# Eleven warm-up products, a Toeplitz load on another queue and five steps moved in a two-layer gated block on one core

## The reference

```python
x = x + tanh(g_xattn[0]) * L0_xattn(ctx, ctx, layernorm(x), ssm_kernel, D, 8)
x = x + tanh(g_ffn[0]) * L0_ffn(layernorm(x), w1, w2, w3)      # hidden 1408
x = x + tanh(g_xattn[1]) * L1_xattn(layernorm(x), ctx, mask)
x = x + tanh(g_ffn[1]) * L1_ffn(layernorm(x), w1, w2, w3)      # hidden 2048
```

## Time and profile before

| what | us |
|---|---|
| median of 3 executions | 703.06 (702.85 to 703.75) |
| the profiled execution, its own time | 704.2 |
| its span, first to last instruction | 702.1 |
| PE busy | 691.6 |
| VectorE busy | 587.6 |
| ScalarE busy | 378.3 |
| GpSimd busy | 270.9 |

### The profile page before, as it was taken

How to read it: one execution, slowest core, us unless ns; L and a number is a source line. 1 busy time by engine, 2 the same in 40 slices (tenths; PEclk the granted TensorE clock), 3 DMA queues, 4 the chain that set the end, 5 groups by cost and what they waited for, 6 DMA issues and landing times.

```text
span 702.1 us, 9602 instructions
## 1 busy us (share of the span) xinstructions
PE 691.6 (99%) x3228; PEld 394.6 (56%) x3228; DVE 587.6 (84%) x1066; ACT 378.3 (54%) x574; POOL 270.9 (39%) x413
## 2 busy tenths in 40 slices
PE   9999999999999999999999999999999999999997
PEld 8777777777544444567654444444444444444445
DVE  4998888999999998658976999888988888888891
ACT  3255885383569898748477544344344334434340
POOL 5779778888766563546600001111100111110000
PEclk9999999999999999999999999999999999999999
DMA  8763464434179889998150434343422334331234
GB/s 293 252 219 116 127 243 132 149 114 121 38 150 193 184 190 193 211 311 345 38 144 15 61 76 90 91 90 76 90 50 57 91 90 91 76 80 44 72 77 106
DMA packets 140593, 90.98 MB, mean 130 GB/s; under 512 B 119040, under 2 KB 119552, under 8 KB 140544
## 3 DMA queue, kind: packets, MB, share of 16 engines
q1 hardware_dynamic: 138816, 86.35, 46.7%
q0 software_dynamic: 1200, 3.93, 1.8%
q10 hardware_dynamic: 528, 0.09, 0.1%
HBM read 53.04 MB, written 8.47 MB: 88 GB/s over the span
## 4 chain that ended last, share of the span: by engine, by line
PE 75%; DVE 10%; POOL 4%; issue 3%; DMA 3%; ACT 3%; SPq 1%; POOLq 0%; ACTq 0%; DVEq 0%
PE psum L854 28%; PE psum L699 15%; PE psum L886 14%; PE psum L781 5%; PE psum L837 3%; PE psum L793 3%; PE psum L815 3%; DMA phase_space<-phase_space 1%; DMA x_sb<-x_between 1%; DVE ln_bn L277 1%; PE psum L870 1%; PE psum L711 1%; DVE phase_space L1309 1%; DMA phase_space<-in_ctx 1%; DVE phase_space L1203 1%
## 5 line engine op out<-in xcount | busy, mean ns | idle before, releaser
L854 PE MATMUL psum<-phase_space 128*128 128x512 f16 x1024 | 223.9, 379 | 1.2 <-DMA phase_space<-phase_space 1.1
L854 PEld LDWEIGHTS psum<-phase_space 128*128 128x128 f16 x1024 | 99.9, 98 | 123.6 <-issue 1.7
L699 PE MATMUL psum<-phase_space 128*128 128x288 f32 x640 | 161.1, 407 | 0.2
L699 PEld LDWEIGHTS psum<-phase_space 128*128 128x128 f32 x640 | 119.0, 190 | 31.3 <-ACT phase_space L960 1.2
L675 POOL DMA_DIRECT2D out<-x_sb x15 | 9.3, 620 | 303.4 <-DVE x_sb L1390 303.4
L886 PE MATMUL psum<-phase_space 128*128 128x512 f16 x480 | 105.7, 379 | 0.0
L1150 ACT ACTIVATE phase_space<-psum,b_scalars 128x512 f32<-128x512 f32 x64 | 43.5, 682 | 80.1 <-PE psum L854 78.1
L781 PE MATMUL psum<-phase_space 128*128 128x512 bf16 (+1 forms) x384 | 79.0, 361 | 0.5 <-DVE phase_space L1251 0.5
L886 PEld LDWEIGHTS psum<-phase_space 128*128 128x128 f16 x480 | 47.0, 98 | 56.6
L1156 ACT ACTIVATE phase_space<-phase_space,magic 128x1024 f32<-128x1024 f32 x32 | 36.4, 1148 | 77.2 <-DVE phase_space L1369 77.2
L1354 DVE SCALAR_TENSOR_TENSOR phase_space<-psum,b_scalars,phase_space 128x512 f32<-128x512 f32 x64 | 47.7, 747 | 25.4 <-ACT phase_space L1150 25.4
(11 more groups left out here) (120 smaller groups left out, 1019.6 us busy)
## 6 DMA issues: line engine op xcount, KB each, us to landing
phase_space<-in_L_weights SPq DMA_DIRECT2D x24, 512.0 KB, 5.8
phase_space<-in_L_weights SPq DMA_DIRECT2D x12, 704.0 KB, 7.3
phase_space<-kpad SPq DMA_DIRECT2D x14, 512.0 KB, 4.2
phase_space<-in_context_heads SPq DMA_DIRECT2D x15, 384.0 KB, 5.2
x_sb<-in_x_tiles SPq DMA_DIRECT2D x16, 256.0 KB, 4.8
phase_space<-in_context_turned SPq DMA_DIRECT2D x8, 512.0 KB, 6.5
x_between<-x_sb SPq DMA_DIRECT2D x16, 256.0 KB
x_sb<-x_between SPq DMA_DIRECT2D x16, 256.0 KB, 7.5
```

The source lines that it names most:

```text
L699: return nc.tensor.matmul(at(bank(4 * hh + lo), 0, [[64, B], [1, NP]]), toep[n % 2][:, hh, (lo - li) * P:(lo - li + 1) * P], kv[n % 2][:, ...
L854: last = nc.tensor.matmul(bank(2 * (m % 3) + w), fb_qT[n % 2][:, kk % 2, kk // 2, :], b_wT[w][:, kk // 2, c * 512:(c + 1) * 512], start=(k ...
```

## The change

It has these parts.

- `warm_up` runs 11 constant products in place of 17.
- The first Toeplitz half is issued by ScalarE's queue as its first load, and d_first by SP in the place that the half had. The order of the other loads stays.
- On ScalarE, in tile 1 of the first FFN, silu (1,1) stands ahead of the rounding of hidden tile 0 instead of behind it.
- Sign chunk 11 moves from the end of stage 1 (`NBA` 12 to 11) to behind the exp of step 0 of stage 2.
- SP issues memories 0 and 1 ahead of the turn of hidden tile 15 instead of behind it and the store of tile 13.
- VectorE's statistics of tile 15 of stage 2 move from step 9 to step 10.
- The down product of tile 0 of the last stage, with the wait for all signs, stands after the chunks of tile 1 instead of tile 2. The down product of tile 1 stays after tile 3.

```diff
@@ -313,10 +313,10 @@
         B_FFN = {1: 5, 3: 6, 5: 7, 7: 8, 8: 9, 9: 10, 10: 11, 11: 12, 12: 13, 13: 14}
         ROWS_FFN = {0: 0, 2: 1, 4: 2, 6: 3, 14: 4}
         RELOAD_FFN = {11: (0,), 12: (1,), 13: (2,), 14: (3,), 15: (4, 5)}
-        NBA = 12
-        SIGN_STEP = {3: 12, 5: 13, 6: 14, 7: 15, 8: 16, 13: 17, 15: 18}
+        NBA = 11
+        SIGN_STEP = {0: 11, 3: 12, 5: 13, 6: 14, 7: 15, 8: 16, 13: 17, 15: 18}
         C_EARLY = {13: (0,), 14: (1, 2), 15: (3,)}
-        C_STEP = {0: (4,), 1: (5,), 2: (6,), 3: (7,), 5: (8,), 6: (9, 10), 7: (11, 12), 8: (13, 14), 9: (15,)}
+        C_STEP = {0: (4,), 1: (5,), 2: (6,), 3: (7,), 5: (8,), 6: (9, 10), 7: (11, 12), 8: (13, 14), 10: (15,)}
         VALID_STEP = {7: 0, 9: 1}
         NEG_STEP = {4: 0, 6: 1, 8: 2, 10: 3}
 
@@ -348,11 +348,6 @@
                     rows = (kpad if n >= 2 else taps_in)[n * G:n * G + G, :]
                     sp.dma_start(toep[n % 2], bass.AP(rows.tensor, rows.offset, [[1, P], [TAP, G], [1, L]])
                                  ).then_inc(s_tp[n % 2], 16)
-
-                def load_first_toeplitz(hh, s_done):
-                    row = taps_in[hh:hh + 1, :]
-                    sp.dma_start(toep[0][:, hh, :], bass.AP(row.tensor, row.offset, [[1, P], [1, L]])
-                                 ).then_inc(s_done, 16)
 
                 def load_weight(w, j):
                     if w == 2:
@@ -415,10 +410,12 @@
                     sp.dma_start(at_mem[b], ctx_in[b].rearrange("(u p) l -> p u l", p=P)).then_inc(c_mem[b], 16)
 
                 sp.dma_start(cx_sb[0][:, 0:NCX // 2], cx[0][:, 0:NCX // 2]).then_inc(s_cfirst, 16)
-                load_first_toeplitz(0, s_tfirst)
+                sp.dma_start(d_first[:, :], dskip[0:2 * G].rearrange("(a n) -> a n", a=1).to_broadcast([P, 2 * G])
+                             ).then_inc(s_tfirst, 16)
                 sp.dma_start(cx_sb[0][:, NCX // 2:NCX], cx[0][:, NCX // 2:NCX]).then_inc(s_cx[0], 16)
                 load_x(0)
-                load_first_toeplitz(1, s_tp[0])
+                row = taps_in[1:2, :]
+                sp.dma_start(toep[0][:, 1, :], bass.AP(row.tensor, row.offset, [[1, P], [1, L]])).then_inc(s_tp[0], 16)
                 load_x(1)
                 load_context(1)
                 load_toeplitz(1)
@@ -447,6 +444,9 @@
                         turn_x(n + 2 - NT)
 
                 for t in range(NT + 1):
+                    if t == NT:
+                        load_memory(0)
+                        load_memory(1)
                     if t >= 1:
                         turn_hidden(t - 1)
                     if t < NT - 2:
@@ -459,9 +459,7 @@
                         load_b(B_FFN[t])
                     for i in RELOAD_FFN.get(t, ()):
                         reload(i)
-                load_memory(0)
                 reload(6)
-                load_memory(1)
                 store_between(NT - 2)
                 store_between(NT - 1)
                 reload(7)
@@ -707,7 +705,7 @@
 
                 def warm_up():
                     pe.wait_ge(s_const, 2)
-                    for _ in range(17):
+                    for _ in range(11):
                         nc.tensor.matmul(bank(7)[:, 0:P], ones[:, :], ones[:, :], start=True, stop=True)
 
                 def first_conv():
@@ -935,9 +933,10 @@
                         pe.wait_ge(g_xT[n % 2], 16 * (n // 2 + 1))
                     for c in range(2 if n == 0 else 0, NCB):
                         b_chunk(n, c)
-                    if n == 2:
+                    if n == 1:
                         pe.wait_ge(s_bs, NBC)
-                    if 2 <= n < NT - 2:
+                        b_down(0)
+                    if 3 <= n < NT - 2:
                         b_down(n - 2)
                     if n == 2:
                         pe.wait_ge(t_red, 2)
@@ -1071,8 +1070,8 @@
                         act.wait_ge(g_xT[n % 2], 16 * (n // 2))
                     nc.scalar.activation(fb_qp[n % 2][:, 0, :], fb_q[n % 2], ACT.Copy).then_inc(g_hi, 1)
 
-                act.dma_start(d_first[:, :], dskip[0:2 * G].rearrange("(a n) -> a n", a=1).to_broadcast([P, 2 * G])
-                              ).then_inc(s_tfirst, 16)
+                row = taps_in[0:1, :]
+                act.dma_start(toep[0][:, 0, :], bass.AP(row.tensor, row.offset, [[1, P], [1, L]])).then_inc(s_tfirst, 16)
                 square_first(0)
                 square_first(1)
                 act.dma_start(kp_sb, taps_in).then_inc(s_kin, 16)
@@ -1110,9 +1109,11 @@
 
                 for t in range(NT):
                     a_silu(t, 0)
-                    if t >= 1:
+                    if t >= 2:
                         a_round_h(t - 1)
                     a_silu(t, 1)
+                    if t == 1:
+                        a_round_h(0)
                     if 1 <= t < NT - 2:
                         a_round_x(t + 2)
                     a_silu(t, 2)
```

## The result

The changed kernel takes 711.32 us, the median of 6 runs (710.62 to 714.17), against 703.12 (702.85 to 703.99, 6 runs) for the kernel before: ratio 1.0121, 95% interval 1.0103 to 1.014. It is slower by 8.2, where 3.9 was forecast, and 711.3 lies above the range.

The account below looks back on a forecast made before the run. TensorE bounds the kernel, busy 691.6 of 702.1 us, so only its gaps count. -0.65-0.65+2.1-0.44+3.5=+3.9: 708.1 us profiled, 706.9 as a median; range 703.6 to 709.8.

Parts of the forecast that it names:

- The start: First stage: shorter warm-up and earlier Toeplitz half start TensorE 0.6 sooner; -0.65 us, ends 0 and -1.3.
- The silu: Tile 1, first FFN: silu fits ScalarE's idle time, its chain ends sooner and closes the 210.31 gap; -0.65 us.
- Sign chunk and memories: Around 293 to 305 us: copy gap shrinks, but memories queued ahead delay the turn of hidden tile 15; +2.1 us net.
- so it waits about 3.2: 0.7 won, 3.2 lost, 0.39 won: Before down product 15: TensorE waits for the late tile, less gaps won at the copy and at 305.10; net +2.1 us.
- Statistics of tile 15: Stage 2: one statistics pair leaves VectorE's busy stretch, closing the gap ended by the exp; -0.44 us, ends -0.44 and 0.
- The early down product: Last stage: TensorE waits 1.7 for hidden tile 0, and the turn of x 3 moves by 3.5; +3.5 us.
- the 2.5 at which the forecast was to fall: Last stage: the forecast falls if the gaps near 392 and before tile 3 sum to less than 2.5 us.
- The four parts that gain: Start -0.65, silu -0.65, sign chunk 0.7 won at the copy, statistics of tile 15 -0.44 us.
- Rival 3: Start: shorter warm-up leaves TensorE idle, first convolution partly at half pace; up to 3.4 us more, 710.3; chance 0.09.
- Rival 1: First FFN: memories do not hold the turn of hidden tile 15; that part -0.4, sum +1.2, 704.3 us; chance 0.14.

Follow-up runs that it names:

- the wait is filled: Changed kernel with the last stage's first down product back behind tile 2, plus 12 constant products ahead of down product 15 of the first FFN: 703.68 us.
- the three fills: Changed kernel with 12, 11 and 12 constant products at the waits before down product 15, the early down product and tile 3: 709.14 us, ratio 1.0081.

## Why the prediction was wrong

**The start** (forecast -0.65): -0.62 by the end of the first stage, but in part by luck. The first convolution started 0.30 sooner (7.04, ended by GpSimd's pairs) and not 0.6, and VectorE's first products 0.22 sooner. The remaining 0.4 is a wait of PE's at 28.67 in the profiled execution of before:

```profile
28.67 0.63 PE L688 MATMUL psum<-ident,phase_space 128*128 128x128 f32 x4 [0.45 <-DVE phase_space L1212]
```

It is absent after the change, but also in the runs with the silu alone and with the down product alone, which leave the start as it was. The Toeplitz move, from which half a microsecond was expected, gives 0.1 of 1.6. The counts of 5 and 6 in the earlier trace rows are not the pace either, since a matmul counts in every stretch that it touches; the 1.3 for the removed matmuls held (5.07 for 6.38).

**The silu** (-0.65): 0.76 in the profile and 1.1 alone. The reasoning for the gap at 192, and the new wait at the first down product (0.63 for "about 0.5"), held. That the gap at 210 hangs on the silu's chain was wrong: it closed with the warm-up alone, where the chain is as it was.

**Sign chunk and memories** (+2.1): the mechanism was right, a wait of 2.75 for the 3.2 forecast, landing 6.0 after issue for the 6.5 of the earlier trace rows. What failed is the step "so it waits about 3.2: 0.7 won, 3.2 lost, 0.39 won": it prices a wait at its own length and puts the matmuls behind it at full pace without a reason. Down product 15 ran at the 1.2 GHz level behind it, 1.55 more. By medians the memories cost 3.7 (704.99 against 701.27), of which 2.4 are left when the wait is filled (703.68); the prediction has 3.2 less 0.39, 2.8. The 0.7 of the sign chunk did not come alone (703.86).

**Statistics of tile 15** (-0.44): the gap closed and nothing replaced it; 0.73 in the profile, and 0.9 alone, with an interval (0.1 to 1.4) that takes in the 0.44.

**The early down product** (+3.5): 5.9 in the profile, 5.6 alone, and 6.8 by medians in the version without the early memories. The two gaps came to 5.3, far from the 2.5 at which the forecast was to fall. PE waits 2.47 for the 1.7 forecast, because the second pair lands in up to 3.5 and not in the 2.7 that was taken. The rest is the same failed step: 1.68 of slow matmuls, which push the scales, the low halves and the turn of x 3 as well. The wait before tile 3 was forecast at 2.7 and is 2.79.

**The sum.** The four parts that gain came out as forecast in their sum, -2.4 by medians for -2.4 (-0.65-0.65-0.7-0.44). Part of that is luck, since singly they measured 1.6, 1.1, nothing and 0.9. The miss of 4.3 is in the other two: 3.7 for 2.8 and 6.8 for 3.5. The step that failed is the same in both. No term held the matmuls that run at half pace behind a wait of more than 2 us, 1.55 and 1.68 in the profile; by medians the three fills take back 2.2 to 2.7.

As a sum from the profile: of the other terms the waits of the last stage came out 0.9 larger than forecast (2.47+1.73 for 1.7+1.64), the wait at down product 15 0.45 smaller, and the gains 0.5 larger (3.3 for 2.8). From 3.9 these lead to 7.1, within 0.4 of the 6.7 of the span. The step from 6.8 to 8.2 is the place of the two profiled executions among their own runs: the prediction took 1.1 off on both sides, but the changed kernel's profiled execution lies 0.3 below its median. Rival 3 had the mechanism, but only at the start, where it decided nothing (the first convolution takes 5.09 for 5.02). Rival 1 adds up to +1.4 and not +1.2, which changes nothing.

The rows to see it were there: the kernel before has no wait over 1.06 on which to read the clock, but its last matmul ends at 698.0 and its own table then reads:

```profile
701.00:702.00 1.00, 0.00 (x0) 0.00 (x0) 0.00 (x0) 0.00 (x0) 0.00 (x0) 1.00 0.00 0
702.00:703.00 1.00, 0.00 (x0) 0.00 (x0) 0.00 (x0) 0.00 (x0) 0.00 (x0) 0.66 0.00 0
703.00:704.00 1.00, 0.00 (x0) 0.00 (x0) 0.00 (x0) 0.00 (x0) 0.00 (x0) 0.50 0.02 8
```

The clock falls some 4.3 us after TensorE stops; in the run with one early memory it took about 2.6 (from 695.3 to 697.9). A forecast that makes new waits of about 3 should have held a rival in which it falls behind each of them, priced from that level: by estimate, a 512-column matmul at twice the 0.22 of the earlier trace rows.

The Trainium skill, "TensorE: Matmul & The Clock Gate", Part 1, states the two levels of 1.2 and 2.4 GHz, and that the moment of the rise varies from run to run with where in the hardware's free-running cycle the first matmul falls. The traces agree as to the pace: the 22 warm-up matmuls take 5.07 in the changed kernel and 4.09 with the shorter warm-up alone, though the granted clock reads 1.00 in both. The fall varies as well: a wait of about 2.8 is followed by level 1.00 in one execution and by 7 us at 0.50 in another.

## What to carry to other kernels

On a kernel that TensorE bounds, price a new wait of two or three microseconds at up to twice its length, as this case measured it (2.77 of wait and 2.96 of slow matmuls at worst): it may lower the clock for what follows, and it did so in some executions only, so the spread of the runs and their mean clock show it before the median does. Before a transfer is hurried, count what its queue already owes; the second 512 KB ahead of a tile that was just in time cost 2.0 us of landing, and a gap of one microsecond was one issue slot of the queue's engine. Gains that close the same gap do not add, so measure each alone before they are summed.

## What was not expected of the hardware

- The clock fell behind waits of 2.09 to 2.81 us, and in one execution did not behind one of 2.79. The lower level lasted some 3.4 us in most cases and 7 in one. In the version with the memories back it fell at about 392.5, 0.8 after PE had taken up its work again.
- 24 constant matmuls in a wait, whose results nobody reads, made the median 1.3 faster.
- The same turned tile took 5.3 to land in some kernels and 3.2 in others, with the same transfers issued just ahead of it. The cause stays open.
